# Three bf16 products of constants ahead of each slot's sum, in the first two of three graph-attention layers

## The chip, the cores and the metric

The kernel runs on one core of one Trainium2 chip. Its metric is the device time of one execution in microseconds (us). A core has a matrix engine (TensorE, PE in the profile, with PEld for its weight loads), VectorE (DVE), ScalarE (ACT), GpSimd (POOL) and SyncE (SP, which only issues DMAs here). They run side by side and wait for each other by semaphores.

## The reference

Three layers of graph attention over 3125 nodes of 256 features and 53125 edges that are sorted by target node, cut here to what matters:

```python
def gat_layer(x, src, dst, W, a_src, a_dst, bias, heads, out_ch):
    xW = (x @ W).reshape(n, heads, out_ch)
    alpha_s = jnp.sum(xW * a_src, axis=-1)
    alpha_d = jnp.sum(xW * a_dst, axis=-1)
    e = jax.nn.leaky_relu(alpha_s[src] + alpha_d[dst], SLOPE)
    m = jax.ops.segment_max(e, dst, num_segments=n)
    w = jnp.exp(e - m[dst])
    z = jax.ops.segment_sum(w, dst, num_segments=n)
    alpha = w / z[dst]
    out = jax.ops.segment_sum(xW[src] * alpha[:, :, None], dst, num_segments=n)
    return out.reshape(n, heads * out_ch) + bias
...
h = jax.nn.elu(gat_layer(x, src, dst, W1, a_src1, a_dst1, b1, H, C))
return gat_layer(h, src, dst, W2, a_src2, a_dst2, b2, 1, F_DIM)
...
x = _layernorm(x + _L0_gnn_ref(...), axis=-1)
x = _layernorm(x + _L1_gnn_ref(...), axis=-1)
```

The first two layers (4 heads of 64, then 1 head of 256) add a self loop to each node. The third (8 heads of 32) adds a term of three edge features to the score instead.

## The kernel before

**Tiling.** The edges are cut into tiles of 128. A slot is one tile against one block of 128 target nodes; there are 440 slots per layer, in 40 batches of 11 (`B`), numbered 0 to 10 within a batch. Everything about a slot sits in SBUF in rings of three batches (`RING`): `rows` (the gathered rows of the source nodes, 264 columns in the first layer, 258 in the second), `onehot` (which edge belongs to which target) and its transpose `onehotT`.

**What happens to a slot.** POOL fetches the slot's 128 rows with an indirect DMA (`gather`, L1271) into the place of the batch three before. ACT or DVE multiplies the rows with the softmax weights (`mul`, L1481 and L828; `OWNER` says whose slot it is: in the first layer ACT has 7 of 11, in the second ACT has 10 and DVE has slot 0). PE sums the edges of each target with one fp32 matmul (`sum_slot`, L1775; the profile shows it as two MATMUL records), whose result goes to one of four PSUM banks, bank 3 to 6 in turn. DVE adds it to the node's total (`add`, L839).

**The weights of the next batches** are made meanwhile, in small steps that are placed between the slots by the hand-written table `AT`. On PE these are: `hot` (six and five bf16 transposes, L1696), `endsT` (L1735 to L1739), `cols` (L1746, waits for ACT's `link`), `factor` (L1755), `adst` (11 bf16 products, L1709), `weightsT` (L1763, L1766) and `scoresT` (L1726). PE takes its instructions strictly in the order in which they are written. In the first layer that order is, with Sn for the sum of slot n: S0 S1 hot S2 endsT hot S3 S4 cols factor S5 S6 adst S7 weightsT S8 S9 scoresT S10. In the second it is: S0 hot S1 endsT hot S2 S3 S4 cols factor S5 adst S6 S7 weightsT S8 scoresT S9 S10.

**What lets POOL go on.** The places of `rows` come free by the count `agg` of finished sums, in three groups (`GATHERS`): the gathers of slots 0 to 3 wait for S3 of the batch three before, those of slots 4 to 7 for S7, those of slots 8 to 10 for S10. So while PE sums batch t, POOL gathers batch t+3.

**The waits of a sum** stand in this order in `sum_slot`: for slot 0 the one-hot matrix (`hotT`); the multiplied rows (`weighted`); and the bank, which is free when DVE's addition of the slot four before is done (`add`). A sum of the first layer uses columns 0 to 263 of its bank, one of the second columns 0 to 257. Each bank has 512 fp32 columns. `ident` is an fp32 identity of 128x128, `identb` the same in bf16; both are written once at the start and only read later.

The third layer has its own order (`small` ahead of `sum_slot`, faces of edge features by `encode`, L1787 and L1794) and only two banks for sums.

Of the kernel before, what the change touches and what calls it, by code (L numbers as in the profile page):

```python
# [22 lines left out]
BF16 = mybir.dt.bfloat16  # L23
# [35 lines left out]
VMAX, RMAX = max(VALS), max(ROW)  # L59
# [16 lines left out]
SOON = 17  # L76
CLEARED = ((0, 6), (6, B), (B, 18), (18, BLOCKS))
AHEAD = 11


PEN_F, PEN_B, PEN_L, PEN_R, START = range(5)
# [35 lines left out]
def gat_kernel(nc, x, src, dst, edge_attr, w1, as1, ad1, b1, w2, as2, ad2, b2, w3, as3, ad3, edge_w, edge_b, b3, out):  # L117
    ctx = ExitStack()
    with ctx:
        def sb(name, shape, dt=F32):  # L120
            return ctx.enter_context(nc.sbuf_tensor(name, shape, dt))
# [52 lines left out]
        ident = sb("ident", [P, P])  # L174
        identb = sb("identb", [P, P], BF16)
# [88 lines left out]
        ps_sum = ([bank[i] for i in (3, 4, 5, 6)], [bank[i] for i in (3, 4, 5, 6)], [bank[i] for i in (3, 4)])  # L264
# [59 lines left out]
        def need(eng, name, count):  # L324

            if isinstance(count, int) and count <= 0:
                return
            eng.wait_ge(ev[name], count + SEED)
# [15 lines left out]
        def done(inst, name):  # L344
            return inst.then_inc(ev[name], 1)
# [19 lines left out]
        def weighted(eng, l, k, s):  # L365

            e = OWNER[l][s]
            before = sum(K * len(OWN[i][e]) for i in range(l))
            need(eng, {"V": "mulv", "A": "mula", "P": "mulp"}[e],
                 before + k * len(OWN[l][e]) + OWN[l][e].index(s) + 1)  # L370
# [15 lines left out]
        def sum_bank(l, t, s):  # L386

            return ps_sum[l][(t.k * B + s) % len(ps_sum[l])]
# [23 lines left out]
        def _(dve):  # L412
# [147 lines left out]
            def statistics(blocks, first):  # L560

                for b in blocks:
                    need(dve, "sum", first + b + 1)
                    done(v.bn_stats(stats[:, b % 2, :], nodes[:, b, :]), "stat")  # L564
                for b in blocks:
                    need(dve, "stat", first + b + 1)
                    done(v.bn_aggr(meanvar[:, b, :], stats[:, b % 2, :]), "aggr")  # L567
# [61 lines left out]
            def residual2(b):  # L629
                need(dve, "scl", b + 1)  # L630
                a = sums[:, b * VALS[2]:(b + 1) * VALS[2]].rearrange("p (h c) -> p h c", h=8)[:, :, 0:CH[2]]
                t = nodes[:, b, :].rearrange("p (h c) -> p h c", h=8)
                done(v.tensor_tensor(t, t, a, ALU.add), "sum")  # L633
# [387 lines left out]
            for two in twos + [range(0)]:  # L1021
                for b in two:
                    if b >= AHEAD:
                        residual2(b)
                if two and two[-1] >= AHEAD:
                    statistics(two, BLOCKS)
# [571 lines left out]
        def _(pe):  # L1598
            m = nc.tensor
# [80 lines left out]
            for l in range(3):  # L1680
# [77 lines left out]
                def weightsT(t, l=l, H=H):  # L1758
# [7 lines left out]
                        m_ = m.transpose(ps_e[:, QT:QT + H * B], expT[0:H * B, 1, :], ident[0:H * B, 0:H * B])  # L1766
                    done(m_, "wp")

                def sum_slot(t, s, l=l, VV=VV):
                    i = (l * K + t.k) * B + s  # L1770
                    if s == 0:
                        need(pe, "hotT", 2 * (l * K + t.k) + 2)
                    weighted(pe, l, t.k, s)
                    need(pe, "add", i + 1 - len(ps_sum[l]))
                    done(m.matmul(sum_bank(l, t, s)[:, 0:VV], onehot[:, t.u, s, :], rows[:, t.u, s, 0:VV],  # L1775
                                  start=True, stop=True), "agg")

# [43 lines left out]
                def period(t, left, l=l):  # L1821
                    n3, n4 = t.after(3), t.after(4)
                    if left > 3 and l < 2:
                        load(n3)
                    for s in range(B):
                        if l == 2:
                            small(t, s, left)
                        sum_slot(t, s)
                        if l < 2:
                            small(t, s, left)  # L1830
                            if left == 1:
                                rows_through(l + 1, (s - 5,))
                            continue
                        if t.k == 0 and s == 5:
                            load(n3)
                        for p, k, i in faces(t.k):
                            if p == s:
                                encode(Batch(k // RING, k % RING), i)
                        if left > 4 and s == B - 1:
                            load(n4)  # L1840
# [67 lines left out]
```

How the kernel before makes its waits and increments, by code:

```python
        def need(eng, name, count):  # L324
            if isinstance(count, int) and count <= 0:
                return
            eng.wait_ge(ev[name], count + SEED)
# [1 line left out]
        def need_apart(eng, *waits):  # L330
            for w, c in waits:
                if isinstance(w, str):
                    need(eng, w, c)
                else:
                    eng.wait_ge(w, c)
# [6 lines left out]
        def done(inst, name):  # L344
            return inst.then_inc(ev[name], 1)
# [14 lines left out]
        def table_written(eng, l):  # L360
            for u in range(TROW):
                eng.wait_ge(s_tab[l][u], 16 * len(range(u, BLOCKS, TROW)))
# [47 lines left out]
        @block.vector  # L411
# [7 lines left out]
            def ch(inst):  # L419
                step[0] += 1
                inst.then_inc(p_dve, 1)
                dve.wait_ge(p_dve, step[0])
                return step[0]
# [11 lines left out]
            def products(l):
                H = HEADS[l]
                dve.wait_ge(s_avec[l], 32)
                for i in range(2):
                    ch(v.tensor_tensor(wprod, wts[l][:, :, 0:D],
                                       avec[l][:, i, :].unsqueeze(1).to_broadcast([P, 2, D]), ALU.mult))
                    ch(v.tensor_reduce(wts[l][:, :, D + i * H:D + (i + 1) * H],
                                       wprod.rearrange("p c (h n) -> p c h n", h=H), AX.X, ALU.add))
            dve.wait_ge(s_dst, 48)
            ch(v.tensor_scalar(dst_allf, dst_all, FAR, None, ALU.subtract))
            dve.wait_ge(p_pool, 6)
            for i, e in enumerate((0, TILES - 1)):
```

## Time and profile before

| | |
|---|---|
| device time, 3 runs | 2488.91 us median (2488.14 to 2496.96) |
| span of the profiled execution, first to last instruction | 2493.9 us |
| PE busy | 1779.5 us, 71% of the span, 9241 matmuls |
| DVE busy | 1586.0 us, 64% |
| POOL busy | 1504.0 us, 60% |
| ACT busy | 1366.9 us, 55% |
| mean granted TensorE clock | 0.770 of 2.4 GHz |
| DMA queue of the gathers (q0) | 181.33 MB, 26.9% of 16 engines |

The page gives the profiled execution's span and no other time of it; the span is 5.0 us (0.2%) above the median of the runs. No engine is busy all the time, so what bounds the kernel has to be read from who waits for whom. The tables below show the TensorE clock as a share: 1.00 is 2.4 GHz and 0.50 is 1.2 GHz, and a value between them is a mix of the two over the stretch. The records of PE are modelled at their ends, and an engine named "remote" as a releaser means that the profile shows no instruction that released the waiting one.

By the starts of the batches, the first layer's steady part lasts from 137 to 720 us, the second's from 891 to 1490 us, and the third layer follows from about 1650 us.

### The profile page before, as it was taken

What the parts mean: (1) busy time and instruction counts of PE and PEld (TensorE: products, weight loads), DVE (VectorE), ACT (ScalarE), POOL (GpSimd) and SP (SyncE); (2) the same over time, 40 slices, a digit from 0 to 9 for tenths busy, and PEclk for the clock granted to TensorE, in tenths of its full rate; (3) what the DMA queues carried; (4) which work ended last, traced back from release to release, by engine and by line L of the source; (5) the groups of instructions that cost most, each with busy time, mean ns of one, the idle gap of its engine ahead of it and who ended that gap; (6) DMA issues with size and microseconds to landing.
All of it is one profiled execution on the core that took longest, in us unless ns stands there. A gap on an engine that the chain in (4) does not pass through costs nothing. (4 is left out here: it accounts for less than half of the span.)

```text
span 2493.9 us, 43223 instructions
## 1 busy us (share of the span) xinstructions
PE 1779.5 (71%) x9241; PEld 1123.8 (45%) x9241; DVE 1586.0 (64%) x4409; ACT 1366.9 (55%) x5004; POOL 1504.0 (60%) x1648
## 2 busy tenths in 40 slices
PE   6267767676766277776776767558888887878874
PEld 5144445444444144444444444335555555555542
DVE  4466666666668155555554556657777777877777
ACT  3255565556556144334344446536676667767666
POOL 3666666666657556656656663626666666766663
PEclk9576676767678566667777677768999989989886
DMA  6644444445531334434433531323433433433331
GB/s 175 160 124 121 115 122 123 118 117 156 144 84 58 97 105 109 111 106 110 112 106 110 164 101 37 113 59 100 114 108 109 117 112 107 114 107 108 107 89 52
DMA packets 130635, 274.39 MB, mean 110 GB/s; under 512 B 39700, under 2 KB 65273, under 8 KB 130366
## 3 DMA queue, kind: packets, MB, share of 16 engines
q0 software_dynamic: 64128, 181.33, 26.9%
q1 hardware_dynamic: 61564, 86.45, 11.6%
q10 hardware_dynamic: 4699, 3.86, 0.6%
q8 instruction: 92, 1.51, 0.2%
q14 instruction: 152, 1.25, 0.2%
HBM read 255.00 MB, written 17.20 MB: 109 GB/s over the span
## 5 line engine op out<-in xcount | busy, mean ns | idle before, releaser
L1271 POOL DMA_INDIRECT rows<-table,index_all x1320 | 1287.8, 976 | 833.2 <-PE bank L1775 383.8
L1775 PE MATMUL bank<-rows,onehot 128*128 128x264 f32 (+1 forms) x2640 | 1089.8, 529 | 290.1 <-ACT rows L1481 156.3
L839 DVE TENSOR_TENSOR sums<-sums,bank 128x264 f32 (+1 forms) x1320 | 555.7, 421 | 465.8 <-PE bank L1775 202.8
L1481 ACT ACTIVATE rows<-rows,wgt 128x33 f32<-128x33 f32 (+2 forms) x3120 | 809.6, 344 | 1.2 <-issue 1.1
L1775 PEld LDWEIGHTS bank<-rows,onehot 128*128 128x128 f32 x2640 | 557.9, 247 | 461.7 <-issue 204.7
L1433 ACT CAST onehot<-bank 128x768 f32<-128x768 bf16 x240 | 177.7, 742 | 301.5 <-remote 174.4
L1489 ACT ACTIVATE prod<-bank 128x512 f32<-128x512 f32 x240 | 133.6, 557 | 244.5 <-PE bank L1787 126.2
L1794 PE MATMUL bank<-late,onehotT 128*128 x1320 | 202.1, 291 | 1.1 <-DVE prod L848 1.1
L848 DVE TENSOR_TENSOR prod<-prod,bank 128x512 f32<-128x512 f32 x240 | 152.4, 635 | 50.3 <-remote 27.4
L857 DVE TENSOR_REDUCE dots<-prod 128x16 f32<-128x512 f32 x240 | 151.7, 632 | 0.5
L1696 PE MATMUL bank<-identb,onehotT 128*128 128x128 bf16 x1320 | 138.3, 251 | 16.6 <-issue 10.0
L1794 PEld LDWEIGHTS bank<-late,onehotT 128*128 128x128 bf16 x1320 | 115.5, 102 | 71.0 <-issue 51.2
L1440 ACT COPY scoreT<-bank 44x256 f32<-44x256 f32 (+2 forms) x120 | 39.2, 327 | 191.1 <-issue 82.5
L828 DVE TENSOR_TENSOR rows<-rows,wgt 128x260 f32<-128x260 f32 (+2 forms) x280 | 120.0, 429 | 35.6 <-ACT wgt L1474 35.6
L1746 PE MATMUL bank<-ones,linkrow 1*44 1x1 f32 (+2 forms) x480 | 47.2, 198 | 130.5 <-ACT linkrow L1450 127.8
L1696 PEld LDWEIGHTS bank<-identb,onehotT 128*128 128x128 bf16 x1320 | 107.7, 114 | 46.7 <-issue 29.2
L1472 ACT COPY rows<-bank 128x44 f32<-128x44 f32 (+1 forms) x80 | 16.4, 205 | 200.0 <-PE bank L1766 159.9
L1746 PEld LDWEIGHTS bank<-ones,linkrow 1*44 1x44 f32 (+2 forms) x480 | 36.6, 140 | 187.3 <-ACT linkrow L1450 160.0
L776 DVE TENSOR_TENSOR_SCAN runs<-chain,bank 1x48 f32<-1x48 f32 (+2 forms) x120 | 29.4, 245 | 142.9 <-remote 139.6
L1283 POOL TENSOR_TENSOR rows<-rows,wgt 128x264 f32<-128x264 f32 x160 | 97.3, 643 | 30.7 <-ACT wgt L1474 30.1
L1787 PE MATMUL bank<-edgew,late 30*128 30x256 bf16 x440 | 96.3, 294 | 14.1 <-ACT prod L1489 8.4
L1726 PE MATMUL bank<-ident,score 128*44 128x128 f32 (+1 forms) x160 | 41.2, 351 | 87.0 <-DVE score L742 69.4
(208 smaller groups left out, 2018.0 us busy)
## 6 DMA issues: line engine op xcount, KB each, us to landing
locb<-loc_d SPq DMA_DIRECT2D x120, 352.0 KB
rows<-table,index_all POOLq DMA_INDIRECT x1320
flags<-flags_d SPq DMA_DIRECT2D x508, 27.5 KB
table<-rows SPq DMA_DIRECT2D x25, 136.0 KB, 1.8
table<-rows SPq DMA_DIRECT2D x25, 134.0 KB
late<-table SPq DMA_DIRECT2D x1, 3300.0 KB
table<-rows SPq DMA_DIRECT2D x25, 129.5 KB, 2.3
late<-table SPq DMA_DIRECT2D x1, 3212.5 KB
```

The lines of the kernel that those rows point to most:

```text
L828: done(v.tensor_tensor(r, r, w.to_broadcast([P, H, n]), ALU.mult), "mulv")
L839: done(v.tensor_tensor(a, a, sum_bank(l, t, s)[:, 0:VV], ALU.add), "add")
L848: done(v.tensor_tensor(prod[:, i % 2, 0:w], prod[:, i % 2, 0:w], ps_hdst[i % 2][:, 0:w], ALU.mult), "prod")
L857: done(v.tensor_reduce(dots[:, t.u, :, lo:hi].rearrange("p h s -> p s h"), prod[:, i % 2, 0:(hi - lo) * D].rearrange("p (s h c) -> p s h c ...
L1271: g.indirect_dma_start(out=rows[:, t.u, s, 0:ROW[l]], out_offset=None, in_=table[l], in_offset=bass.IndirectOffsetOnAxis(ap=index_all[:, t ...
L1283: done(g.tensor_tensor(r, r, w.to_broadcast([P, H, n]), ALU.mult), "mulp")
L1433: done(a.copy(onehot[:, t.u, lo:hi, :].rearrange("p s e -> p (s e)"), ps_hotb[l][g][:, 0:(hi - lo) * P]), "hotT")
L1481: i = a.activation(r, r, ACT.Copy, scale=wgt[:, t.u, h * B + s:h * B + s + 1])
L1489: done(a.activation(prod[:, i % 2, 0:w], ps_enc[:, 0:w], ACT.Relu), "enc")
L1696: r = m.transpose(ps_hotb[l][g][:, (s - lo) * P:(s - lo + 1) * P], onehotT[:, t.u, s * P:(s + 1) * P], identb[:, :])
L1775: done(m.matmul(sum_bank(l, t, s)[:, 0:VV], onehot[:, t.u, s, :], rows[:, t.u, s, 0:VV], start=True, stop=True), "agg")
L1794: r = m.matmul(ps_hdst[i % 2][:, (s - lo) * D:(s - lo + 1) * D], onehotT[:, t.u, s * P:(s + 1) * P], hnode3[:, bass.ds(b, 1), j, :].rearra ...
```

## The change

`sum_slot` now waits for the bank first. Then, in the first two layers, PE writes three products of bf16 constants into columns 264 to 511 of that bank (248 columns each: stationary `identb`, moving the bits of `ident` read as bf16), and only then waits for the multiplied rows and makes the sum. Nothing reads what the products write. No semaphore is signalled by them.

```diff
+SPARE = 3
...
+                def keep_busy(b, n):
+
+                    for _ in range(n):
+                        m.matmul(b[:, VMAX:512], identb[:, :], ident[:, :].bitcast(BF16)[:, 0:512 - VMAX],
+                                 start=True, stop=True)
+
                 def sum_slot(t, s, l=l, VV=VV):
                     i = (l * K + t.k) * B + s
                     if s == 0:
                         need(pe, "hotT", 2 * (l * K + t.k) + 2)
+                    need(pe, "add", i + 1 - len(ps_sum[l]))
+                    if l < 2:
+                        keep_busy(sum_bank(l, t, s), SPARE)
                     weighted(pe, l, t.k, s)
-                    need(pe, "add", i + 1 - len(ps_sum[l]))
                     done(m.matmul(sum_bank(l, t, s)[:, 0:VV], onehot[:, t.u, s, :], rows[:, t.u, s, 0:VV],
                                   start=True, stop=True), "agg")
```

The order of PE's instructions around `cols` shows where the products come to stand. In these rows L1773 is a product, L1775 and L1784 are the sum before and after, L1746/L1747 is `cols`, L1755/L1756 is `factor`, and the first rows of `adst` are L1708/L1709 (a register step) and L1709/L1710. First PE in the first layer, from S3 to the start of `adst`, before:

```order
L1775 MATMUL bank<-rows,onehot 128x264 [waits ev_add,ev_mula]
L1775 MATMUL bank<-rows,onehot 128x264 [waits ev_add,ev_mulv]
L1746 MATMUL bank<-ones,linkrow 44x1 [waits ev_link]
L1746 MATMUL bank<-ones,linkrow 44x1
L1755 MATMUL bank<-scale,carry 128x4 [waits ev_w,ev_sc1,ev_resc,ev_rscale]
L1775 MATMUL bank<-rows,onehot 128x264 [waits ev_add,ev_mula] x2
```

and with the change, from S4 to S5:

```order
L1773 MATMUL bank<-ident,identb 128x248 [waits ev_add]
L1773 MATMUL bank<-ident,identb 128x248 x2
L1784 MATMUL bank<-rows,onehot 128x264 [waits ev_mulv]
L1747 MATMUL bank<-ones,linkrow 44x1 [waits ev_link]
L1747 MATMUL bank<-ones,linkrow 44x1
L1756 MATMUL bank<-scale,carry 128x4 [waits ev_w,ev_sc1,ev_resc,ev_rscale]
L1773 MATMUL bank<-ident,identb 128x248 [waits ev_add]
L1773 MATMUL bank<-ident,identb 128x248 x2
L1784 MATMUL bank<-rows,onehot 128x264 [waits ev_mula]
```

The products of S4 stand ahead of the wait for `link`, those of S5 behind it. In the second layer PE had, from S6 to S8:

```order
L1775 MATMUL bank<-rows,onehot 128x258 [waits ev_add,ev_mula] x2
L1763 MATMUL bank<-ident,expT 128x11 [waits ev_w,ev_exp]
L1766 MATMUL bank<-ident,expT 128x11 [waits ev_mask]
L1775 MATMUL bank<-rows,onehot 128x258 [waits ev_add,ev_mula]
```

and now has, from S6 to `weightsT`:

```order
L1773 MATMUL bank<-ident,identb 128x248 [waits ev_add]
L1773 MATMUL bank<-ident,identb 128x248 x2
L1784 MATMUL bank<-rows,onehot 128x258 [waits ev_mula]
L1773 MATMUL bank<-ident,identb 128x248 [waits ev_add]
L1773 MATMUL bank<-ident,identb 128x248 x2
L1784 MATMUL bank<-rows,onehot 128x258 [waits ev_mula]
L1764 MATMUL bank<-ident,expT 128x11 [waits ev_w,ev_exp]
L1767 MATMUL bank<-ident,expT 128x11 [waits ev_mask]
```

S6 and S7, which stood back to back, each have three products ahead of them. No instruction of another engine is added, removed or moved.

## Rows read from the trace of the kernel before

**Rows 1.** Busy time by stretch: steady part of layers 1 and 2, then two single batches.

```profile
core 0: us, PE busy (x) PEld busy (x) DVE busy (x) ACT busy (x) POOL busy (x), PEclk, DMA share, GB/s
137.16:720.19 583.03, 415.94 (x2030) 272.27 (x2030) 366.11 (x1109) 344.84 (x1331) 378.39 (x386) 0.71 0.45 125
891.39:1489.91 598.52, 432.79 (x2030) 263.99 (x2030) 307.38 (x983) 245.84 (x701) 364.68 (x386) 0.70 0.41 114
...
403.87:420.64 16.77, 13.84 (x58) 9.09 (x58) 10.27 (x32) 9.94 (x39) 10.68 (x12) 0.59 0.44 119
...
470.73:487.45 16.72, 10.48 (x58) 6.89 (x58) 10.33 (x33) 9.92 (x39) 10.65 (x11) 0.81 0.45 120
```

**Rows 2.** Timeline of POOL, first layer: start, length, line, idle before and releaser.

```profile
434.33 0.95 POOL L1271 DMA_INDIRECT rows<-table,index_all  x1 [0.30 <-issue]
437.40 0.94 POOL L1271 DMA_INDIRECT rows<-table,index_all  x1 [2.12 <-remote]
...
443.42 0.94 POOL L1271 DMA_INDIRECT rows<-table,index_all  x1 [1.19 <-PE bank L1775]
```

**Rows 3.** Timeline of PE, first layer: S3 and S4, cols, S5 and S6, S7.

```profile
433.13 1.11 PE L1775 MATMUL bank<-rows,onehot 128*128 128x264 f32 x4
438.20 0.32 PE L1746 MATMUL bank<-ones,linkrow 1*44 1x1 f32 x4 [3.96 <-ACT linkrow L1450]
...
439.05 2.13 PE L1775 MATMUL bank<-rows,onehot 128*128 128x264 f32 x4
...
441.31 1.23 PE L1775 MATMUL bank<-rows,onehot 128*128 128x264 f32 x2
```

**Rows 4.** Timeline of DVE, the same batch: the addition of slot 2.

```profile
437.05 0.43 DVE L839 TENSOR_TENSOR sums<-sums,bank 128x264 f32 x1 [3.98 <-remote]
```

**Rows 5.** PE by stretches of 1 us around that moment: busy, clock, DMA share, GB/s.

```profile
436.00:437.00 1.00, 0.00 (x0) 1.00 0.40 116
437.00:438.00 1.00, 0.00 (x0) 1.00 0.00 0
```

**Rows 6.** Timeline of PE, second layer: S2 and S3, S4, S6 and S7.

```profile
1144.97 1.09 PE L1775 MATMUL bank<-rows,onehot 128*128 128x258 f32 x4
1149.97 1.23 PE L1775 MATMUL bank<-rows,onehot 128*128 128x258 f32 x2 [3.91 <-ACT rows L1481]
...
1153.19 2.07 PE L1775 MATMUL bank<-rows,onehot 128*128 128x258 f32 x4
```

**Rows 7.** Timeline of POOL, second layer: the gather that waits for S7.

```profile
1155.53 0.95 POOL L1271 DMA_INDIRECT rows<-table,index_all  x1 [2.22 <-PE bank L1775]
```

**Rows 8.** PE by stretches of 2 us behind the pause: busy, clock, DMA share, GB/s.

```profile
438.20:440.20 2.00, 1.98 (x9) 0.58 0.26 69
...
444.20:446.20 2.00, 1.73 (x6) 0.72 0.41 104
...
1149.97:1151.97 2.00, 2.00 (x9) 0.50 0.48 122
...
1153.97:1155.97 2.00, 2.00 (x7) 0.67 0.31 81
```

**Rows 9.** Third layer: two stretches with their clock, then six bf16 matmuls of 256 columns in each.

```profile
1898.00:1904.00 6.00, 5.34 (x42) 3.62 (x42) 4.82 (x13) 3.81 (x17) 5.21 (x8) 1.00 0.26 70
1930.00:1934.00 4.00, 4.00 (x17) 2.33 (x15) 3.25 (x8) 3.31 (x13) 2.94 (x3) 0.57 0.45 105
...
1900.39 0.83 PE L1794 MATMUL bank<-late,onehotT 128*128 x6
1901.06 1.11 PE L1709 MATMUL bank<-dtab,onehotT 128*128 x11
...
1932.29 1.42 PE L1794 MATMUL bank<-late,onehotT 128*128 x6
1933.55 0.61 PE L1775 MATMUL bank<-rows,onehot 128*128 128x264 f32 x2
```

**Rows 10.** Busy time by stretch: the batches at the ends of layers 1 and 2, without gathers.

```profile
720.19:755.80 35.61, 24.41 (x120) 16.06 (x121) 25.19 (x78) 21.59 (x90) 14.83 (x18) 0.79 0.17 44
...
1489.91:1527.20 37.29, 29.29 (x122) 18.10 (x123) 20.94 (x68) 16.07 (x51) 10.39 (x11) 0.64 0.15 40
```

## The prediction

> **What bounds the kernel now.** I first read the busy times by stretch, one row per layer. The steady part of the first layer takes 583.03 us for 35 batches, 16.66 us each, and of the second 598.52 us, 17.10 us each [rows 1]. PE is busy for 71 to 72% of both, at a mean clock of 0.71 and 0.70. That invites the thought that a faster clock would help, so I next compared two single batches of the first layer: at clock 0.59 one takes 16.77 us, at 0.81 another takes 16.72 us [rows 1]. In the first layer the clock moves PE's busy time from 13.84 to 10.48 us and the batch not at all.
>
> What repeats with the batch is POOL. It issues eleven gathers, about 1.25 us from start to start (0.95 of work and 0.30 of issue), and stops twice [rows 2]. The stop ahead of slot 0 (2.12 us) waits for S3, the stop ahead of slot 4 (1.19 us) for S7. At the first stop PE's records say that S3 and S4 were over at 434.24 (433.13 + 1.11) [rows 3], yet DVE adds slot 2 only at 437.05, POOL goes on at 437.40 and PE at 438.20 [rows 2 to 4]. In between the DMA engines fall from a share of 0.40 to 0.00 [rows 5]. I take it that the signals came through only when the gathered data had landed; the trace names no releaser. So PE pauses for about 4 us in each batch, and S3 has 2.8 us to spare. In the second layer S4 waits 3.91 us for ACT's product after the same moment [rows 6].
>
> The stop for S7 is different. In the second layer S7 ends at 1155.26 (1153.19 + 2.07) and the gather starts 0.27 us later, after 2.22 us of idling [rows 6, 7]: PE's chain from the end of its pause to S7 sets this gather. The chain runs without a gap from 1149.97 to 1155.26, 5.29 us. In the first layer S7 ends at 442.54 (441.31 + 1.23) and the gather starts 0.88 us later [rows 2, 3], so S7 has 0.88 - 0.27 = 0.6 us to spare.
>
> **The price of a product.** No row shows a bf16 matmul of 248 columns in these layers. The nearest are the matmuls of 256 columns in the third: six take 0.67 us to the next line's start at full clock (0.11 each) and 1.26 us at half clock (0.21 each) [rows 9]. That gives 3.6 us (full) or 6.9 us (half) for the 33 products of a batch. The bounds of what they cost the batch are nothing (all in PE's waits) and these sums.
>
> **Where they are covered.** The nine products ahead of S2 to S4 run in PE's pause, or in the 2.8 us that S3 has to spare; in the second layer S4's stand ahead of its wait for ACT. Those ahead of S8 to S1 have the waits for `scoresT` and the next weights, and nothing of POOL's hangs on them unless they add over 1 us. I cost both at nothing. If the pause went, S3 would be late next. The bank's wait now stands ahead of the rows' wait, but it asks for the addition four slots back, and whoever waits for the sum needed both anyway: nothing.
>
> **Where they are not.** Nine products stand behind the pause and ahead of S7: those of S5, S6 and S7. At half clock they are 1.9 us, at full clock 1.0 us. Which it is depends on the clock behind the pause. Now it is 0.58 and 0.50 there, and full clock is back after some 5 to 7 us of unbroken work: in the second layer near 1155.3, in the first near 445.3 [rows 8]. The pause ahead stays in the first layer, since DVE's addition and `link` end it and the products of S5 stand behind `link`. So I expect half clock for 5 us and full clock behind.
>
> - *Second layer.* 5.29 + 1.9 = 7.2 us of half-clock work: 5.0 at half clock, the other 2.2 in 1.1, so 6.1 us against 5.29 in this row; some batches now have a faster chain (the mean of 17.10 us is below this batch's), so I take +1.0 us per batch.
> - *First layer.* From 438.20 to 442.54 is 4.34 us; with 1.9 it is 6.2, of which 5.0 at half clock and 1.2 in 0.6: 5.6 us, 1.3 later, less the 0.6 to spare: +0.65 us.
>
> POOL's two stops come in 37 batches of each layer (3 of 40 are gathered ahead), so 37 x (0.65 + 1.0) = 61 us. At the layers' ends PE is busy for 24.41 of 35.61 us and for 29.29 of 37.29 us [rows 10]; the 66 products of such a stretch are 7 to 14 us, the idle time 11 and 8 us; I take 2 and 3 us, 5 in all. The third layer has no products. Sum: 66 us on the span of 2493.9, which stands 5.0 us above the median; I carry no difference for that and put the sum on the median: 2488.9 + 66 = 2555 us.
>
> **A rule that speaks against the change.** The sums are issued in order behind the products, and in the rows no later matmul starts ahead of an earlier one [rows 3, 6]. The Trainium skill ("TensorE: Matmul & The Clock Gate", the section on packing small matmuls) says the same: matmuls start and end in program order. If sums could overtake the products, the 61 us would be none and the time 2489.
>
> **The rivals.**
>
> *A. The clock stays at full speed (faster).* PE's work between pauses is denser, and the products ahead of S3 and S4 shorten the pause. If the clock no longer fell, S7 would be early: S3 and S4 take 1.11 us at full clock where S5 and S6 take 2.13 at half [rows 3], so the second layer's 5.29 becomes about 2.9, with nine products 3.9. POOL's stop then falls from 2.22 to the 1.19 that the first layer shows, the batch from about 17.25 (this row's) to 16.2: 37 x (17.10 - 16.2) = 33 us. The first layer gains nothing, by its two batches at 0.59 and 0.81. That gives 2457 us. It decides when half clock behind the pause lasts under about 2 us. Against it: the pause of 3.9 to 4.0 us is longer than the 2 us or so of products that fit into it, and half clock follows it in the rows. The Trainium skill (same page, section "Why this matters for your kernels") would have TensorE kept busy without long gaps to hold the full clock; the trace agrees that pauses precede half clock, and the rule gives rival A only if the products close the pause.
>
> *B. Half clock all the way to S7 (slower still).* Then 1.3 us in the first layer and 1.9 plus 0.2 in the second: 37 x 3.4 = 126, with 10 at the ends 2625 us. For it: in the first layer half clock lasts 7 us now. Against it: the products leave fewer gaps.
>
> *C. No change.* The half-clock stretch gives back in quicker sums what the products take; or the products are absorbed by waits that the records do not show, as the signals held back at 437. Then 2489, give or take 12.
>
> That PE leaves the products out can be excluded: the order shows them, 3 x 880 = 2640 instructions.
>
> **How the numbers follow.** Forecast 0.60, A 0.13, B 0.12, C 0.15. A measurement of this kernel can tell 0.5%, 12 us, from no change. Faster: A and a little of C, 0.15. Same: 0.13. Slower: 0.72. The range from 2475 to 2600 takes in C and the forecast with its terms between half and one and a half, and leaves out most of A and of B.
>
> **What would show it.** Right: batches of about 17.3 and 18.1 us; POOL's stop for S7 near 1.8 us in the first layer and near 3.2 in the second, released by the sum; its other stop unchanged; half clock at the end of the pause; a mean clock near 0.85 in both layers. Wrong: a clock at or near 1.00 there with a stop for S7 near 1.2 us (A), or unchanged batches (C). A product that takes over 0.25 us, or a late S3, would break the prices.

## The result, and the profile after

The changed kernel takes 2624.8 us (median of 4 runs, 2609.83 to 2656.32) beside 2488.52 us (4 runs, 2488.07 to 2496.96) for the kernel before: ratio 1.0506, 95% interval 1.0464 to 1.0549. The ratio leaves out one slow run of the changed kernel (2656.32 us), which the medians count. By the medians it is slower by 136 us, twice the 66 us of the forecast; the time lies outside the forecast's range. Of two later comparisons one gave 1.0616 (1.0595 to 1.0638), the other 1.0508 (1.0462 to 1.0554).

The page of the changed kernel begins (to be read against the table of the time before):

```profile
span 2608.0 us, 47705 instructions
...
PE 1927.6 (74%) x11881; PEld 1262.1 (48%) x11881; DVE 1591.2 (61%) x4409; ACT 1362.7 (52%) x5004; POOL 1504.9 (58%) x1648
```

The 2640 products are there. PE is busy for 148 us more, its weight loads for 138 us, and no other engine's busy time moved by more than 6 us. The stretches that answer to [rows 1], 35 batches of the first and of the second layer:

```profile
138.64:775.92 637.28, 474.75 (x3185) 327.01 (x3185) 371.29 (x1111) 343.62 (x1331) 375.19 (x386) 0.87 0.42 115
...
950.92:1607.83 656.91, 501.25 (x3186) 330.10 (x3185) 306.62 (x978) 242.10 (x697) 366.99 (x386) 0.84 0.38 104
```

The batches take 18.2 and 18.8 us instead of 16.7 and 17.1. These two stretches grew by 54.3 and 58.4 us, 112.6 of the 114.1 us between the two profiled spans (the profiled execution of the changed kernel was the quickest of its four). The mean clock rose from 0.71 and 0.70 to 0.87 and 0.84, and the time rose with it.

Since POOL's gathers set the batch, the view that tells most is the gathers' group over one layer's steady part: busy time, mean ns of one, and after the second bar the idle time ahead of them with what ended it. Before, first and second layer:

```profile
L1271 POOL DMA_INDIRECT rows<-table,index_all x408 | 401.0, 983 | 228.0 <-issue 100.2 <-PE bank L1775 76.2 <-remote 51.6
...
L1271 POOL DMA_INDIRECT rows<-table,index_all x408 | 386.5, 947 | 258.8 <-PE bank L1775 129.3 <-issue 102.0 <-remote 27.4
```

and after:

```profile
L1272 POOL DMA_INDIRECT rows<-table,index_all x407 | 396.5, 974 | 285.8 <-PE bank L1784 171.0 <-issue 98.5 <-remote 16.3
...
L1272 POOL DMA_INDIRECT rows<-table,index_all x407 | 388.2, 954 | 317.6 <-PE bank L1784 217.3 <-issue 100.3
```

A gather is as long as before and its issue as well. The idle time grew by 57.8 and 58.8 us, 116.6 in all, and that is the whole loss between the two spans. Averaged over the 37 batches of a layer that have stops (0.30 us of each stop is issue, and the first stop of a layer, 13 to 15 us, is in the mean), the stop for S3 (ahead of slot 0's gather) went from 2.28 to 3.00 us in the first layer and from 2.17 to 3.72 in the second; the stop for S7 from 1.13 to 1.70 and from 2.03 to 2.12; the idle time ahead of slot 8, for S10, from 0.30 to 0.59 in the first layer and not at all in the second. So most of the loss is a late S3: 37 x (0.72 + 1.55) = 84 us. The forecast had left that stop as it was.

**How S3 comes late, second layer.** One batch of the changed kernel, first on PE: S0 and the first hot group, then, with a cut between, the products of S3 and S3 itself. The columns are start, length, engine, line, what, count, and the idle time ahead.

```profile
1411.86 0.60 PE L1784 MATMUL bank<-rows,onehot 128*128 128x258 f32 x2
1412.30 0.50 PE L1697 MATMUL bank<-identb,onehotT 128*128 128x128 bf16 x6
...
1414.77 0.48 PE L1773 MATMUL bank<-ident,identb 128*128 128x248 bf16 x3
1418.31 0.70 PE L1784 MATMUL bank<-rows,onehot 128*128 128x258 f32 x2 [3.06 <-ACT rows L1482]
```

ACT, the same batch: the copy of the first hot group, the multiplication of slot 3, the copy of the second.

```profile
1417.04 0.80 ACT L1434 CAST onehot<-bank 128x768 f32<-128x768 bf16 x1 [6.25 <-remote]
1417.74 0.51 ACT L1482 ACTIVATE rows<-rows,wgt 128x257 f32<-128x257 f32 x1
1418.15 0.68 ACT L1434 CAST onehot<-bank 128x640 f32<-128x640 bf16 x1
```

POOL, the last gather ahead of the stop, and the two stops:

```profile
1414.64 0.94 POOL L1272 DMA_INDIRECT rows<-table,index_all  x1 [0.31 <-issue]
1419.28 0.95 POOL L1272 DMA_INDIRECT rows<-table,index_all  x1 [3.69 <-PE bank L1784]
...
1426.84 0.95 POOL L1272 DMA_INDIRECT rows<-table,index_all  x1 [2.85 <-PE bank L1784]
```

The first hot group is over by PE's record at 1412.80, but ACT's copy of it starts at 1417.04, 4.24 us later. In ACT's order slot 3's multiplication stands behind that copy, S3 behind the multiplication, and the gather behind S3: 1419.01 + 0.27. The DMA engines fall silent at the moment at which the copy starts:

```profile
1416.50:1417.00 0.50, 0.00 (x0) 0.00 (x0) 0.00 (x0) 0.00 (x0) 0.00 (x0) 1.00 0.40 141
1417.00:1417.50 0.50, 0.00 (x0) 0.00 (x0) 0.24 (x2) 0.46 (x1) 0.00 (x0) 1.00 0.00 0
```

That is the release of [rows 4, 5] again. The kernel before has it too, but there it catches only the second copy. ACT of before, the batch of [rows 6]:

```profile
1143.91 0.80 ACT L1433 CAST onehot<-bank 128x768 f32<-128x768 bf16 x1 [1.94 <-PE bank L1696]
1144.61 0.51 ACT L1481 ACTIVATE rows<-rows,wgt 128x257 f32<-128x257 f32 x1
1148.30 0.69 ACT L1433 CAST onehot<-bank 128x640 f32<-128x640 bf16 x1 [3.18 <-remote]
```

There the first copy follows the hot group by 0.19 us (1143.72 to 1143.91; the mean over the layer is 0.10). So slot 3 is multiplied at 1144.61, ahead of the held stretch, and S3 runs in time. In the changed kernel the mean lag of the copy is 3.73 us.

**First layer.** There ACT's copies stand behind slot 3's multiplication. In 11 of the 37 batches another link falls into the held stretch. PE of the changed kernel, where `endsT` comes late, and DVE:

```profile
405.08 0.61 PE L1784 MATMUL bank<-rows,onehot 128*128 128x264 f32 x2
408.82 0.19 PE L1736 MATMUL bank<-runs,ones 1*1 1x4 f32 x2 [3.13 <-issue]
```

```profile
407.92 0.43 DVE L840 TENSOR_TENSOR sums<-sums,bank 128x264 f32 x1 [3.22 <-remote]
408.26 0.41 DVE L767 TENSOR_TENSOR_SCAN top<-flags,top 44x128 f32<-44x128 f32 x1
```

DVE's addition waits for a held signal, the scan that `endsT` needs stands behind it, and S3 stands behind `endsT` on PE (S2, at 405.08, is already over). The stop for S3 is 3.30 us there, and 3.8 to 5.7 us in ten other batches of the 37; in all eleven PE idles for 3.1 to 5.4 us ahead of `endsT` and DVE for 2.5 to 5.3 us ahead of that addition. This link is read from the traces alone: no run moved it.

### The profile page after: what moved, and what is told of

Its sections match the earlier page's. It is cut to its first block and busy times, and to the rows that moved or that the text cites. A ratio compares the mean times of both kernels' runs of the same rounds, so it can differ in the third digit from the quotient of the medians.

```text
span 2608.0 us, 47705 instructions
## 1 busy us (share of the span) xinstructions
PE 1927.6 (74%) x11881; PEld 1262.1 (48%) x11881; DVE 1591.2 (61%) x4409; ACT 1362.7 (52%) x5004; POOL 1504.9 (58%) x1648
## 5 line engine op out<-in xcount | busy, mean ns | idle before, releaser
L1784 PE MATMUL bank<-rows,onehot 128*128 128x264 f32 (+1 forms) x2640 | 973.5, 459 | 221.9 <-ACT rows L1482 115.7
L1784 PEld LDWEIGHTS bank<-rows,onehot 128*128 128x128 f32 x2640 | 473.2, 221 | 325.8 <-ACT rows L1482 137.0
L1773 PE MATMUL bank<-ident,identb 128*128 128x248 bf16 x2640 | 490.0, 301 | 27.4 <-issue 24.4
L1773 PEld LDWEIGHTS bank<-ident,identb 128*128 128x128 bf16 x2640 | 250.6, 106 | 149.8 <-issue 78.1
L1697 PE MATMUL bank<-identb,onehotT 128*128 128x128 bf16 x1320 | 128.3, 239 | 15.7 <-issue 9.7
L1697 PEld LDWEIGHTS bank<-identb,onehotT 128*128 128x128 bf16 x1320 | 98.5, 107 | 38.7 <-issue 19.5
L1736 PE MATMUL bank<-runs,ones 1*1 1x4 f32 (+2 forms) x240 | 22.7, 164 | 120.9 <-DVE top L767 96.9
```

The costliest lines, as they stand in the source:

```text
L1697: r = m.transpose(ps_hotb[l][g][:, (s - lo) * P:(s - lo + 1) * P], onehotT[:, t.u, s * P:(s + 1) * P], identb[:, :])
L1773: m.matmul(b[:, VMAX:512], identb[:, :], ident[:, :].bitcast(BF16)[:, 0:512 - VMAX], start=True, stop=True)
```

## The experiments

The ratios are to the kernel before on the same chip, with 95% intervals. Where a diff is shown, everything else is the changed kernel, unless said otherwise.

**The wait alone**, `SPARE = 0`: no products, the bank's wait still first.

> No products; only the wait for the bank stands ahead of the wait for the rows. Every theory here: the sum needed both anyway, so 2489 us within 0.3%, batches of 16.7 and 17.1 us, and the hot transposes' signal reaches ScalarE as in the kernel before (0.04 us behind the record in the second layer). If the moved wait is what costs, it takes part of the 136 us.

2491.62 us, ratio 0.9987 (0.9966 to 1.0009). The moved wait costs nothing.

**Products by slot.** First S5 to S7:

```diff
-                    if l < 2:
+                    if l < 2 and s in (5, 6, 7):
```

> Products only ahead of slots 5, 6 and 7, behind the pause. Theory 'chain to S7' (my prediction's): these cost nearly all, so about 2489 + 61 = 2550 us or more. Theory 'late hot' (products ahead of the hot transposes push them past the moment from which TensorE's signals arrive late): only the S7 stop pays, 0.57 us in the first layer's 37 batches by the changed kernel, little in the second, plus a push of hot where the pause does not absorb it: 2505 to 2535. Theory 'each product costs the same': 3/11 of 136, 2526.

2540.0 us, 1.0185 (1.0152 to 1.0218).

With `s in (8, 9, 10, 0, 1)`:

> Products only ahead of slots 8, 9, 10, 0 and 1, so ahead of the hot transposes. Theory 'chain to S7': nothing, 2489 us. Theory 'late hot': most of the loss, 2550 to 2600 us, with GpSimd's stop ahead of slot 0 grown from 1.9 to 3 us or more in the second layer and ScalarE's copy of hot 2 to 4 us behind the transposes' records. Theory 'each product the same': 5/11 of 136, 2551, with no such sign.

2568.66 us, 1.032 (1.0276 to 1.0365).

With `s in (2, 3, 4)`:

> Products only ahead of slots 2, 3 and 4, behind hot and mostly in the pause. Theory 'late hot' and theory 'chain to S7': no cost, 2489 us, or a few us faster if the clock behind the pause stays at full speed more often. Theory 'each product the same': 3/11 of 136, 2526.

2483.3 us, 0.995 (0.9928 to 0.9971).

The kernel before took 2492.76 us beside these. By the medians the parts are +47, +76 and -9 us, 114 us together, against 126 us (by the ratio) or 136 us (by the medians) for the whole: they nearly add up, and the largest part is the one that I had costed at nothing. The gathers' group with S5 to S7 alone, both layers:

```profile
L1272 POOL DMA_INDIRECT rows<-table,index_all x407 | 398.3, 979 | 244.2 <-issue 101.5 <-remote 73.7 <-PE bank L1784 69.0
...
L1272 POOL DMA_INDIRECT rows<-table,index_all x407 | 386.0, 948 | 286.8 <-PE bank L1784 131.6 <-issue 99.3 <-remote 55.9
```

16 and 28 us more than before, and it is the stop for S7 that grew (1.13 to 1.51 and 2.03 to 2.81 us): the place and the mechanism of the forecast. With S8 to S1 alone:

```profile
L1272 POOL DMA_INDIRECT rows<-table,index_all x407 | 400.9, 985 | 254.7 <-PE bank L1784 130.2 <-issue 97.9 <-remote 26.6
...
L1272 POOL DMA_INDIRECT rows<-table,index_all x407 | 387.4, 952 | 302.8 <-PE bank L1784 202.9 <-issue 99.9
```

27 and 44 us more, and here the stop for S3 grew (2.17 to 4.03 us in the second layer) while that for S7 fell (2.03 to 1.34). With S2 to S4 alone, in the second layer PE and its clock behind the stop for S3:

```profile
1198.47 0.97 PE L1784 MATMUL bank<-rows,onehot 128*128 128x258 f32 x2
...
1200.38 0.70 PE L1784 MATMUL bank<-rows,onehot 128*128 128x258 f32 x2 [0.63 <-ACT rows L1482]
```

```profile
1199.00:1201.00 2.00, 1.37 (x7) 0.55 (x5) 1.65 (x5) 1.97 (x8) 0.99 (x2) 0.95 0.00 0
1201.00:1203.00 2.00, 2.00 (x21) 1.67 (x21) 1.72 (x7) 0.93 (x3) 1.70 (x2) 1.00 0.41 106
```

S4 (1200.38) waits 0.63 us instead of 3.91 [rows 6] (a long one; the median batch of the kernel before has 2.9), and from there to S7 PE runs at full clock, where [rows 8] have 0.50. S3 itself (1198.47) now runs at half clock until past 1199.0 (granted clock 0.50 from 1197.0 to 1199.0) and sets the gather. The two nearly cancel over the layer: the stop for S3 grows from 2.17 to 2.81 us, that for S7 falls from 2.03 to 1.33. In the first layer neither moved by more than 0.1 us (2.34 and 1.17). The gain of 0.5% (9 us by the medians) is clear of the interval, and this trace, from the slowest of the eight runs (2492.3 us), doesn't show where it comes from.

**A second set, in which the kernel before was 16% quicker.** Four kernels followed, and beside them the kernel before took 2100.34 us (13 runs, 2093.9 to 2110.18). Twelve products ahead of slot 4 alone:

```diff
-                    if l < 2:
-                        keep_busy(sum_bank(l, t, s), SPARE)
+                    if l < 2 and s == 4:
+                        keep_busy(sum_bank(l, t, s), 4 * SPARE)
```

> Twelve products ahead of slot 4 alone, in the pause, in the first two layers. In the run with products ahead of slots 2 to 4 the second layer's chain to S7 ran at full clock and its stop for S7 fell to 1.33 us, but its stop for S3 rose to 2.81. If the clock is held by work in the pause and the products of slots 2 and 3 are what made S3 late, then here the stop for S7 stays near 1.3 and that for S3 goes back to 2.2: 37 x 0.7 = 26 us off, about 2463 us. If 1.3 us of products do not hold the clock, no change.

2092.14 us, 0.9952 (0.993 to 0.9974).

The same with `8 * SPARE`, 24 products:

> Twenty-four products ahead of slot 4 alone: 2.6 us at full clock, still within the pause of 4 us. Clock at full speed behind the pause in both layers. As with twelve: about 2463 us; a few us more if the products outlast the pause and make the chain to S7 start late (the first layer's link ends the pause at 438.2 in a batch whose S3 ends at 433.7, so 4.5 us are there).

2166.25 us, 1.0332 (1.0284 to 1.0379).

Two kernels whose gathers in the first two layers bring a quarter (first layer) or a seventh (second) of each row from the fourth batch on, the changed one and the one before. The gather's edit, the same in both:

```diff
-                            g.indirect_dma_start(out=rows[:, t.u, s, 0:ROW[l]], out_offset=None, in_=table[l],
+                            wide, parts = (ROW[l], 1) if l == 2 or not old else ((67, 4), (37, 7))[l]
+                            g.indirect_dma_start(out=rows[:, t.u, s, 0:wide], out_offset=None,
+                                                 in_=table[l].rearrange("a (k c) -> (a k) c", k=parts),
```

> The changed kernel with gathers that bring a quarter (first layer) or a seventh (second layer) of a row from the fourth batch on, so the rows' contents are not the reference's; GpSimd issues as many gathers as before. Theory 'signals wait for gather data': the hot transposes' signal reaches ScalarE within 0.1 us of its record in both layers, the stop for S3 shrinks to what TensorE needs, batches below 17 us. Rival 'signals wait for GpSimd's own work' (descriptor writing): they stay late by 2 to 4 us, and the batch hardly changes.

> The kernel before with the same short gathers (contents not the reference's). Theory 'signals wait for gather data': the first layer's 2.3 us between the hot record and ScalarE's copy falls to 0.1, TensorE's pause of 4 us goes, batches of 14 to 15 us. Rival 'GpSimd's own work': no change in the pause.

2090.28 and 2099.87 us, one run each. These four were meant for the 4 us pause, and it wasn't there: with twelve products the stops for S3 and S7 are 0.3 to 0.4 us, little more than the issue (0.30), and POOL gathers back to back. So they tell nothing of the held signals. The two with narrow gathers moved 93 MB in the gathers' queue instead of 181 and were no quicker, so at this speed the bytes are not the bound; the number of gathers is the same. The other two tell of PE: 24 products (S3 and S7 end 0.27 us ahead of the gather in most first-layer batches) make PE itself the bound, twelve do not.

**The changed kernel and the kernel before once more, with two narrower parts.** The kernel before took 2515.13 us (13 runs).

> The changed kernel once more, unchanged, beside the kernel before. One theory: the 5% are a property of this program, 1.045 to 1.055 wherever it runs. The other: they come from TensorE's late semaphores in front of the stop for S3, which the kernel before shows only where its batches take 16.7 us; on a chip where the kernel before takes about 2100 us its stops are near 0.3 us, and the ratio then lies between 1.00 and 1.03, set by TensorE's own time (33 products of 0.11 to 0.21 us a batch, some 5 us beside a batch of 14 us).

2668.95 us, 1.0616 (1.0595 to 1.0638).

> The kernel before once more, with a profile, so that its stops on this chip stand beside those of the changed kernel. No change: ratio 1.00. If the chip is like that of the first comparison, about 2490 us and batches of 16.7 us with a stop for S3 of 2.2 us; if like the other, about 2100 us, batches near 14 us and stops near 0.3 us.

2511.41 us, one run: its trace is like that of the first comparison, with stops for S3 of 2.43 and 2.31 us.

Products only ahead of the three slots that are farthest from the stop for S3, `s in (8, 9, 10)`:

> Products ahead of S8, S9 and S10 alone. If the hot groups are late because of whatever stands ahead of them, these nine products put off the first hot group by 1 to 2 us and S3 with it: where the kernel before takes about 2490 us, 40 to 80 us more (ratio 1.015 to 1.03), the stop for S3 in the second layer from 2.17 to over 3 us. If only the products behind the hot groups, ahead of S0 and S1, put S3 off, ratio within 0.5% of 1. Where the kernel before takes about 2100 us: within 1% of 1 by either.

2554.56 us, 1.0153 (1.0136 to 1.017).

And `s in (0, 1)`:

> Products ahead of S0 and S1 alone, the six nearest the stop for S3. The rival to the run with S8 to S10: if these delay S3, they do so by their own time, 6 x 0.21 = 1.3 us at most and under 0.7 us at full clock, so 15 to 45 us more (ratio 1.006 to 1.018) where the kernel before takes about 2490 us. If the hot groups decide, ratio within 0.5% of 1, and the copy on ScalarE behind the first hot group starts as before, 0.1 us behind its record's end in the second layer. Where the kernel before takes about 2100 us: within 1% of 1.

2517.67 us, 1.0014 (0.9997 to 1.0031). The gathers of the second layer, before in this set, then with S8 to S10:

```profile
L1271 POOL DMA_INDIRECT rows<-table,index_all x408 | 387.3, 949 | 256.9 <-PE bank L1775 118.0 <-issue 101.3 <-remote 37.6
```

```profile
L1272 POOL DMA_INDIRECT rows<-table,index_all x407 | 386.2, 949 | 297.8 <-PE bank L1784 199.3 <-issue 97.2 <-remote 1.4
```

All of the loss is in the second layer (40.9 us; the first layer's gathers idle for 237.8 us against 236.2). ACT's first copy starts 3.85 us behind the hot group's record there, and 1.62 us with S0 and S1 alone, where the stop for S3 grows by 0.39 us and that for S7 gives 0.32 back. The nine products that are farthest from S3 cost 39 us; the six next to it cost nothing that can be told from zero. To stand ahead of the first hot group is not enough, or three are too few: S0's three stand there in the second layer as well, and the copy lags less than half as much. Together (the run with S8 to S1) they cost 76 us against 42 us for the two apart, though on another chip; why is not shown.

**Is it the copy's place?** The second layer's copies one slot later in ACT's order, so that slot 3's multiplication stands ahead of the first:

```diff
-    dict(tops2=0, links=1, finish=5, mask=6, scores=7, tops=10, hot=3, load=8,
-         link=2, exp=7, weights=7, hotT=(0, 1), copy=7,
+    dict(tops2=0, links=1, finish=5, mask=6, scores=7, tops=10, hot=3, load=8,
+         link=2, exp=7, weights=7, hotT=(1, 2), copy=7,
```

> All products as in the change, and in the second layer ScalarE's copies of the hot groups stand one slot later in its order, so that the multiplication of slot 3 no longer stands behind the first copy. If the stop for S3 is long because that copy waits for TensorE's late signal and slot 3's multiplication is queued behind it, the second layer's stop falls from 3.7 to 4.3 us to 2.6 us or less, the next stop grows by at most half of that, and the ratio to the kernel before falls from 1.05 to 1.06 to 1.02 to 1.045 where the kernel before takes about 2500 us. If TensorE itself brings S3 late (its own work and its own late signals), the stop and the ratio stay within 0.5% of the changed kernel's. Where the kernel before takes about 2100 us: no stops of such a length in either, ratio 0.99 to 1.03.

Here the kernel before took 2099.76 us (34 runs), so there was no pause again. 2096.7 us, 0.9975 (0.9956 to 0.9995).

The kernel before with the same edit:

> The kernel before with the same later place of the two copies. There the first copy starts 0.1 us behind the hot group's record in the second layer, so slot 3's multiplication has nothing to wait for: ratio 0.995 to 1.005 by the theory of the late copy; by the rival, that the copy's place is worth something whatever the products, 0.99 or less.

2101.33 us, 0.9997 (0.998 to 1.0014).

With the copies in their old place, products ahead of S2 to S7, `1 < s < 8`:

> Products ahead of S2 to S7, none ahead of the first hot group. If what stands ahead of the hot groups makes the loss beyond S5 to S7's own, the sum of the two single runs holds: 1.0185 and 0.995, that is 1.01 to 1.02 where the kernel before takes about 2500 us, and the stop for S3 stays at 2.2 to 2.8 us. If the number of products decides, six of eleven slots give half of the loss or more: 1.03. Where the kernel before takes about 2100 us, within 1% of 1.

2092.72 us, 0.9962 (0.9945 to 0.9979). The case at 2490 us stays untried, and with it the rival that the number of products decides and not their place; only the runs by slot above speak against it (nine products cost 47, 39 and -9 us by where they stand).

Products ahead of S2 to S4 alone, with the later copies:

> Products ahead of S2 to S4 alone, and the second layer's copies one slot later: a candidate for a version quicker than both. Full clock behind the pause as in the run with S2 to S4 (ratio 0.995), and the stop for S3 in the second layer, 2.81 us there, falls back to 2.2 if the copy held it: ratio 0.985 to 0.99. If the copy has no part in it, 0.995 again. Where the kernel before takes about 2100 us: 0.99 to 1.0.

2093.36 us, 0.996 (0.9944 to 0.9977); at 2490 us untried too.

The last set met the pause again (the kernel before 2489.77 us, 7 runs). The changed kernel, unchanged:

> The changed kernel, unchanged, a third time. Where the kernel before takes about 2500 us: 1.05 to 1.06 as before. Where it takes about 2100 us: 0.99 to 1.00, since all products with ScalarE's later copies gave 0.9975 there; a ratio over 1.01 would mean that the later copies had hidden a loss.

2621.05 us, 1.0508 (1.0462 to 1.0554).

With the later copies:

> All products with ScalarE's later copies, again. Where the kernel before takes about 2500 us: 1.02 to 1.045 and a second-layer stop for S3 of 2.6 us or less if the copy of the first hot group passes the delay on to S3; the changed kernel's ratio within 0.5% and its stop if TensorE itself is late. Where the kernel before takes about 2100 us: equal to the changed kernel within 0.5%.

2583.2 us, 1.0367 (1.0334 to 1.0401). The gathers of the changed kernel in this set, both layers:

```profile
L1272 POOL DMA_INDIRECT rows<-table,index_all x408 | 396.2, 971 | 296.6 <-PE bank L1784 188.0 <-issue 97.2 <-remote 11.4
...
L1272 POOL DMA_INDIRECT rows<-table,index_all x407 | 386.4, 949 | 326.2 <-PE bank L1784 225.0 <-issue 101.1
```

and with the later copies:

```profile
L1272 POOL DMA_INDIRECT rows<-table,index_all x408 | 395.5, 969 | 303.1 <-PE bank L1784 197.5 <-issue 99.6 <-remote 6.0
...
L1272 POOL DMA_INDIRECT rows<-table,index_all x407 | 396.8, 975 | 269.9 <-issue 100.8 <-PE bank L1784 99.4 <-remote 69.7
```

The second layer's idle time falls by 56 us, to within 11 us of the kernel before's, and its stop for S3 from 3.81 to 2.36 us. Its gathers themselves take 10 us more (975 instead of 949 ns each), so the layer's steady part is 45 us shorter. The rest of the program is the same in both; the first layer idles 7 us more in this profiled execution, and the medians differ by 38 us. One batch of the kernel with the later copies, ACT and then POOL:

```profile
1294.53 2.10 ACT L1482 ACTIVATE rows<-rows,wgt 128x257 f32<-128x257 f32 x5
1302.53 0.80 ACT L1434 CAST onehot<-bank 128x768 f32<-128x768 bf16 x1 [5.90 <-remote]
```

```profile
1303.10 0.94 POOL L1272 DMA_INDIRECT rows<-table,index_all  x1 [2.11 <-remote]
```

The copy still waits (the hot group was over at 1298.23), but five multiplications, slot 3's among them, are done ahead of it, and the stop is back at 2.1 us with "remote" as its releaser, as in the kernel before. That shows the second layer's link: a delayed completion, a copy that waits for it, and slot 3's work queued behind the copy. What is left, 1.0367, was not taken apart further; the first layer's stop for S3 is no shorter than in the changed kernel (3.61 and 3.22 us), and the second layer's stop for S7 stands at 2.19 us.

## Why the prediction was wrong

- **Price of a product**: right. In the changed kernel three take 0.32 us to the next line's start at full clock (1411.54 to 1411.86) and 0.62 us at half clock (1424.90 to 1425.52): 0.11 and 0.21 us each.
- **Moved bank wait, nothing**: right (0.9987).
- **Products ahead of S2 to S4, nothing**: nearly right; alone they gain 0.5%. The pause does take them, and the clock behind it is full, which I had only as rival A's condition; the second layer's stop for S7 fell to 1.33 us, near the 1.19 that rival A gave it.
- **"Those ahead of S8 to S1 ... I cost both at nothing"**: this step failed. They cost 3.2% alone, 76 us where the whole costs 136. The argument was that nothing of POOL's hangs on them unless they add over 1 us. It looked at PE's own slack ahead of S3 (2.8 us) and not at the other chain to S3: hot group, ACT's copy, slot 3's multiplication. I had read the held signals as a fixed delay of a fixed set of waits, but which waits they catch depends on where PE's work stands when the hold begins. The copy's lag in the second layer was 0.10 us before and 3.73 after, and the stop for S3 went from 2.17 to 3.72 us. Why the hold begins and ends where it does stays open.
- **Products ahead of S5 to S7, 61 us**: mechanism right, size somewhat high; alone they cost 47 us, with the stop for S7 up by 0.38 and 0.78 us a batch where I had 0.65 and 1.0. Within the whole change the second layer's term nearly vanished (2.03 to 2.12 us), since a POOL that starts its gathers later gives S7 the time.
- **Layer ends, 5 us**: 114.1 - 112.6 leaves 1.5 us for all that lies outside the two steady stretches.
- **Clock 0.85**: right (0.87 and 0.84), and worth nothing by itself.
- **Rivals**: A (2457 us) fell; in the changed kernel the last 0.7 us of PE's work ahead of the gather that waits for S7 ran at full clock in 19 of 36 batches of the first layer and 17 of the second. C fell. B's 2625 us is the measured time by chance alone: its mechanism, half clock all the way to S7, holds in 9 and 13 of the 36 batches only, and would have put 1.3 and 2.1 us into the stop for S7, which grew by 0.57 and 0.09. The text's own warning, that "a late S3 would break the prices", names what happened; I gave it no price and no chance.

The Trainium skill ("TensorE: Matmul & The Clock Gate", the section "Why this matters for your kernels") advises to keep TensorE busy so that its full clock holds. The trace agrees on the clock (0.71 to 0.87 in the first layer), and shows that here the time goes the other way.

## What to carry to other kernels

Filler work on an in-order engine is free only if everything behind it is free: follow each signal that is put off through the queue of the engine that waits for it, and see what stands behind that wait, not only the slack of the engine that got the filler. Where signals come in bursts, a small shift can cost more than itself (here nine products ahead of S8 to S10, 1.0 to 1.9 us a batch, made the copy lag 3.85 us), so place filler behind the last signal that others need and ahead of a wait (S2 to S4 here, 0.5% quicker), and put a copy that waits for such a signal behind work that does not need it. A higher granted clock is no gain where another engine's waits set the time.

## What the runs showed of the hardware

**Completions of TensorE are seen late, in a burst, mostly when the gathers have landed.** In the batches of [rows 2 to 5] and of the second layer above, DVE or ACT goes on within 0.4 us of the moment at which the DMA share falls to 0.00 for good, and the other engines follow. The fall alone is no trigger. In the kernel before, in the batch of [rows 6], the share falls to 0.00 before that too and rises again, and nothing goes on until the last fall:

```profile
1147.10:1147.30 0.20, 0.00 (x0) 0.00 (x0) 0.00 (x0) 0.00 (x0) 0.00 (x0) 1.00 0.00 0
...
1148.10:1148.30 0.20, 0.00 (x0) 0.00 (x0) 0.07 (x1) 0.00 (x1) 0.00 (x0) 1.00 0.01 0
```

And in the first-layer batch of the changed kernel DVE goes on at 407.92 while gathered data is moving:

```profile
407.90:408.10 0.20, 0.00 (x0) 0.00 (x0) 0.18 (x1) 0.00 (x0) 0.20 (x1) 1.00 0.67 236
```

What holds the signals is open: the trace does not tell a late signal from work that ended later than PE's modelled records say. Nor does a simple rule of time fit: in the kernel before the first hot group's signal comes through within 0.2 us when its record ends 2.08 us ahead of the start of the last gather (1143.72 and 1145.80) and at once when it ends 1.1 to 1.3 us ahead, as in most batches; in the changed kernel it is held when it ends 1.84 us ahead (1412.80 and 1414.64).

**The same program ran at two speeds.** The kernel before took 2482 to 2520 us in the first comparison and in three later ones, but 2092 to 2110 us in two others, and one of the chips gave both. Its time in the gathers' queue is the same: 26.9% of 2493.9 us and, with ACT's later copies, 32.0% of 2099.8 us, 671 and 672 us. What differs is the held stretch. The kernel before with the later copies, first layer, at the place that answers to [rows 2 to 4], on DVE, PE and POOL:

```profile
434.67 0.43 DVE L839 TENSOR_TENSOR sums<-sums,bank 128x264 f32 x1 [0.21 <-DVE sums L839]
```

```profile
436.27 0.32 PE L1746 MATMUL bank<-ones,linkrow 1*44 1x1 f32 x4 [0.64 <-ACT linkrow L1450]
```

```profile
434.15 0.94 POOL L1271 DMA_INDIRECT rows<-table,index_all  x1 [0.30 <-issue]
```

DVE waits 0.21 us instead of 3.98, PE 0.64 instead of 3.96, and POOL doesn't stop. At that speed all products together with the later copies gave 0.9975, and those ahead of S2 to S7 0.9962; the unchanged form of the changed kernel was not run there with whole gathers. What makes the one speed or the other stays open. The 5% loss by this change was measured at the slower one alone.
